# Edge loads of 124 rows instead of 128 in a two-layer graph attention kernel

## What is computed

```python
q = (x @ Wq.T + bq).reshape(N, H, C)
k = (x @ Wk.T + bk).reshape(N, H, C)
v = (x @ Wv.T + bv).reshape(N, H, C)
logits = (q[dst] * k[src]).sum(-1) * (1.0 / np.sqrt(C).astype(np.float32))
m = jax.ops.segment_max(logits, dst, num_segments=N)
e = jnp.exp(logits - m[dst])
denom = jax.ops.segment_sum(e, dst, num_segments=N)
alpha = e / (denom[dst] + 1e-16)
msg = v[src] * alpha[..., None]
out = jax.ops.segment_sum(msg, dst, num_segments=N).reshape(N, HC)
return out + x @ Ws.T + bs
```

## Time and profile before

| what | us |
|---|---|
| median of 3 executions | 3700.6 |
| span of the profiled execution | 3707.0 |
| layer 1, first indirect load of kv to the end of the last | 197.1 to 1338.4 |
| layer 2, the same | 1515.0 to 2666.8 |
| experts, from the first load of `fin_x` | 2701.5 to 3707.0 |
| one indirect load of kv: POOL busy, mean | 1.074 |

### The profile page before, as it was taken

How to read it: one execution, slowest core, us unless ns; L and a number is a source line. 1 busy time by engine, 2 the same in 40 slices (tenths; PEclk the granted TensorE clock), 3 DMA queues, 4 the chain that set the end, 5 groups by cost and what they waited for, 6 DMA issues and landing times. The chain is left out here.

```text
span 3707.0 us, 49221 instructions
## 1 busy us (share of the span) xinstructions
PE 2464.8 (66%) x13243; PEld 2115.8 (57%) x13243; DVE 2398.1 (65%) x3615; ACT 1119.3 (30%) x2130; POOL 2051.4 (55%) x1958
## 2 busy tenths in 40 slices
PE   2435556665656656265656556655569999999999
PEld 1324444554545444154544444444459989989898
DVE  3347777777777764277777777777746556566555
ACT  6301111111111111011111111111146666666665
POOL 6567777777777747677777777777610000000000
PEclk9756666666666655566666666666679999999999
DMA  9334444444444422344444445444310000000000
GB/s 378 112 103 119 125 121 122 125 119 128 119 127 119 124 69 71 87 123 136 124 129 127 125 125 132 124 131 125 97 38 4 23 22 3 23 22 2 21 11 11
DMA packets 394181, 356.62 MB, mean 96 GB/s; under 512 B 88694, under 2 KB 327436, under 8 KB 394080
## 3 DMA queue, kind: packets, MB, share of 16 engines
q1 hardware_dynamic: 221360, 168.40, 15.2%
q0 software_dynamic: 62896, 125.63, 13.6%
q10 hardware_dynamic: 109824, 61.36, 5.4%
HBM read 246.90 MB, written 108.30 MB: 96 GB/s over the span
## 5 line engine op out<-in xcount | busy, mean ns | idle before, releaser
L542 POOL DMA_INDIRECT kv<-kv_table,ix x1664 | 1786.4, 1074 | 531.4 <-issue 497.2
L554 PE MATMUL kT<-identity,kv 128*128 128x128 f32 x832 | 361.3, 435 | 1037.6 <-DMA kv<-kv_table,ix 1037.6
L554 PEld LDWEIGHTS kT<-identity,kv 128*128 128x128 f32 x832 | 182.5, 219 | 1061.1 <-DMA kv<-kv_table,ix 813.4
L650 ACT ACTIVATE ex<-gap 128x1024 f32<-128x1024 f32 x208 | 219.8, 1057 | 1859.4 <-DVE gap L626 1859.4
L604 DVE TENSOR_TENSOR_SCAN held_q<-mask,held_q,qT 128x512 f32<-128x512 bf16 x208 | 266.1, 1280 | 600.4 <-PE qT L555 599.5
L1324 DVE TENSOR_TENSOR hid_lo_x<-full_x,hid_hi_x 128x448 fp32r<-128x448 f32 x448 | 276.2, 622 | 267.8 <-ACT hid_hi_x L1210 264.0
L1210 ACT ACTIVATE full_x<-psH_x,offset_x,scale_x 128x448 f32<-128x448 f32 x448 | 332.5, 742 | 290.6 <-PE psH_x L1065 290.5
L561 PE MATMUL logit<-kq,head_sum 128*128 128x512 f32 x416 | 388.7, 1037 | 1.9 <-DVE gap L626 1.9
L1014 POOL DMA_DIRECT2D x_x<-in_x x7 | 6.8, 974 | 633.6 <-DVE total_x L1368 633.6
L555 PE MATMUL qT<-identity,qz 128*128 128x128 f32 x832 | 347.2, 417 | 0.0
L578 PE MATMUL restT<-pick,top 128*128 128x8 f32 x1664 | 335.4, 274 | 0.0
(11 more groups left out here) (209 smaller groups left out, 5238.8 us busy)
## 6 DMA issues: line engine op xcount, KB each, us to landing
running_sums<-rows ACTq DMA_DIRECT2D x208, 288.0 KB
qz<-q_at_starts SPq DMA_DIRECT2D x208, 256.0 KB, 3.2
mask<-masks SPq DMA_DIRECT2D x416, 128.0 KB, 3.7
q_at_starts<-zeros SPq DMA_DIRECT2D x16, 1664.0 KB, 18.7
kv<-kv_table,ix POOLq DMA_INDIRECT x1664
x_sb<-in_x SPq DMA_DIRECT2D x1, 6272.0 KB, 27.3
kv_table<-proj SPq DMA_DIRECT2D x14, 448.0 KB, 3.3
x_x<-in_x POOLq DMA_DIRECT2D x7, 896.0 KB, 5.7
```

Source lines behind the costliest of these rows:

```text
L542: pool.indirect_dma_start(kv[:, u, j, 2 * HC * s:2 * HC * (s + 1)], None, kv_t, bass.IndirectOffsetOnAxis(ix[:, u, n:n + 1], 0), bounds_ch ...
L554: pe.transpose(kT[u % 2][:, P * j:P * (j + 1)], kv[:, u, j, 0::2], identity[:, :])
```

## The change

A tile of edges is ROWS = 124 edges instead of 128, one to a partition, so partitions 124 to 127 of `ix`, `kv`, `qz` and `rows` are not used. TPB stays 4, so a block is 496 edges of each stream. 106250 edges then need 27 turns of four blocks, 108 blocks a layer instead of 104; the loop keeps its 24 turns, and three turns are written out before it instead of two. All tiles of 512 columns in SBUF become 496 wide, and transposes are of 124 rows or to 124 rows; the PSUM banks stay 512 wide. `q_at_starts` has 107136 rows instead of 106496.

```diff
@@ -40,13 +40,15 @@
 assert NG * GROUP == NT and NG % 2 == 1
 
 STREAMS = 2
-STEP = 512
-TPB = STEP // P
+ROWS = 124
+TPB = 4
+STEP = TPB * ROWS
 UNROLL = 4
 BLOCKS = -(-E // (STREAMS * STEP * UNROLL)) * UNROLL
 STEPS = BLOCKS // UNROLL
 HALF = BLOCKS * STEP
 EP = STREAMS * HALF
+QROWS = -(-EP // P) * P
 ROW = HC + 2 * HEADS
 DEN, MAX = HC, HC + HEADS
 
@@ -59,7 +61,8 @@
 PROJ = 4 * HC
 HTOK = GROUP * P // 2
 GTOK = GROUP * P
-assert STEPS - 2 == len(EXPERT_LAYERS) * EXPERTS
+PEELED = STEPS - len(EXPERT_LAYERS) * EXPERTS
+assert PEELED >= 2
 
 
 def each_group(eng, body):
@@ -92,12 +95,12 @@
     kv_t = nc.dram_tensor("kv_table", [NP, 2 * HC], F32, kind="Internal").ap()
     q_t = nc.dram_tensor("q_table", [NP, HC], F32, kind="Internal").ap()
 
-    qz_t = nc.dram_tensor("q_at_starts", [EP, HC], F32, kind="Internal").ap()
+    qz_t = nc.dram_tensor("q_at_starts", [QROWS, HC], F32, kind="Internal").ap()
     sum_t = nc.dram_tensor("running_sums", [EP, ROW], F32, kind="Internal").ap()
     mask_t = nc.dram_tensor("masks", [STREAMS, BLOCKS, 2 * STEP], BF16, kind="Internal").ap()
 
-    qz_blocks = qz_t.rearrange("(b j p s) c -> b p j (s c)", j=TPB, p=P, s=STREAMS)
-    sum_blocks = sum_t.rearrange("(b j p s) c -> b p j (s c)", j=TPB, p=P, s=STREAMS)
+    qz_blocks = qz_t[0:EP, :].rearrange("(b j p s) c -> b p j (s c)", j=TPB, p=ROWS, s=STREAMS)
+    sum_blocks = sum_t.rearrange("(b j p s) c -> b p j (s c)", j=TPB, p=ROWS, s=STREAMS)
     kv_nodes = kv_t.rearrange("(i p) c -> p i c", p=P)
     q_nodes = q_t.rearrange("(i p) c -> p i c", p=P)
 
...
@@ -450,12 +453,12 @@
                     return phase.enter_context(nc.sbuf_tensor(f"{name}_{layer}", shape, dt))
 
                 def pb(name):
-                    return phase.enter_context(nc.psum_tensor(f"{name}_{layer}", [P, STEP], F32))
+                    return phase.enter_context(nc.psum_tensor(f"{name}_{layer}", [P, 512], F32))
 
                 U = UNROLL
-                ix = sb("ix", [P, U, TPB * STREAMS], I32)
-                kv = sb("kv", [P, U, TPB, STREAMS * 2 * HC])
-                qz = sb("qz", [P, U, TPB, STREAMS * HC])
+                ix = sb("ix", [ROWS, U, TPB * STREAMS], I32)
+                kv = sb("kv", [ROWS, U, TPB, STREAMS * 2 * HC])
+                qz = sb("qz", [ROWS, U, TPB, STREAMS * HC])
                 mask = sb("mask", [P, U, 2, STEP], BF16)
                 held_q = sb("held_q", [P, 2, STEP])
                 kq = sb("kq", [P, 2, STEP])
@@ -465,20 +468,20 @@
                 wv = sb("wv", [P, 2, STEP])
                 run_v = sb("run_v", [P, U, STEP])
                 run_d = sb("run_d", [P, U, STEP])
-                rows = sb("rows", [P, 2, TPB, STREAMS, ROW])
+                rows = sb("rows", [ROWS, 2, TPB, STREAMS, ROW])
                 if layer == 1:
                     w_raw = sb("w_raw", [P, KC * HID])
                 kT = [pb(f"kT{i}") for i in range(2)]
                 qT = [pb(f"qT{i}") for i in range(2)]
                 vT, logit, outT = pb("vT"), pb("logit"), pb("outT")
-                restT = pb("restT")[:, 0:2 * TPB * STREAMS * HEADS].rearrange("p (m j h) -> p m j h", m=2, j=TPB)
+                restT = pb("restT")[0:ROWS, 0:2 * TPB * STREAMS * HEADS].rearrange("p (m j h) -> p m j h", m=2, j=TPB)
 
                 block = phase.enter_context(nc.Block())
 
 
 
                 past = STEPS * layer
-                peeled = 2
+                peeled = PEELED
 
                 def each_step(eng, body):
                     for i in range(past, past + peeled):
@@ -551,20 +554,20 @@
                         pe.wait_ge(q_in[u], 16 * i + 16)
                         wait_past(pe, kq_ready, b - 1)
                         for j in range(TPB):
-                            pe.transpose(kT[u % 2][:, P * j:P * (j + 1)], kv[:, u, j, 0::2], identity[:, :])
-                            ins = pe.transpose(qT[u % 2][:, P * j:P * (j + 1)], qz[:, u, j, :], identity[:, :])
+                            pe.transpose(kT[u % 2][:, ROWS * j:ROWS * (j + 1)], kv[:, u, j, 0::2], identity[0:ROWS, 0:ROWS])
+                            ins = pe.transpose(qT[u % 2][:, ROWS * j:ROWS * (j + 1)], qz[:, u, j, :], identity[0:ROWS, 0:ROWS])
                         ins.then_inc(kq_turned, 1)
 
                     def logits(b, u, i):
                         pe.wait_ge(kq_ready, b + 1)
                         wait_past(pe, gaps_ready, b)
-                        pe.matmul(logit[:, :], head_sum[:, :], kq[:, u % 2, :], start=True, stop=True)\
+                        pe.matmul(logit[:, 0:STEP], head_sum[:, :], kq[:, u % 2, :], start=True, stop=True)\
                             .then_inc(logits_ready, 1)
 
                     def turn_v(b, u, i):
                         wait_past(pe, weighted, b)
                         for j in range(TPB):
-                            ins = pe.transpose(vT[:, P * j:P * (j + 1)], kv[:, u, j, 1::2], identity[:, :])
+                            ins = pe.transpose(vT[:, ROWS * j:ROWS * (j + 1)], kv[:, u, j, 1::2], identity[0:ROWS, 0:ROWS])
                         ins.then_inc(v_turned, 1)
 
                     def turn_results(b, u, i):
@@ -572,10 +575,10 @@
                         pe.wait_ge(d_summed, b + 1)
                         wait_past(pe, copied, 3 * b)
                         for j in range(TPB):
-                            of = slice(P * j, P * (j + 1))
-                            pe.transpose(outT[:, of], run_v[:, u, of], identity[:, :])
+                            of = slice(ROWS * j, ROWS * (j + 1))
+                            pe.transpose(outT[0:ROWS, P * j:P * (j + 1)], run_v[:, u, of], identity[:, :])
                             pe.matmul(restT[:, 0, j, :], run_d[:, u, of], pick[:, :], start=True, stop=True)
-                            ins = pe.matmul(restT[:, 1, j, :], top[:, u, 1 + P * j:1 + P * (j + 1)], pick[:, :],
+                            ins = pe.matmul(restT[:, 1, j, :], top[:, u, 1 + ROWS * j:1 + ROWS * (j + 1)], pick[:, :],
                                             start=True, stop=True)
                         ins.then_inc(out_turned, 1)
 
...
@@ -655,7 +658,7 @@
                         act.wait_ge(out_turned, b + 1)
                         wait_past(act, rows_out[h], 16 * (U // 2 * i + u // 2))
                         flat = rows[:, h, :, :, :].rearrange("p j s c -> p (j s) c")
-                        act.activation(flat[:, :, 0:HC], outT[:, :].rearrange("p (r c) -> p r c", c=HC),
+                        act.activation(flat[:, :, 0:HC], outT[0:ROWS, 0:TPB * P].rearrange("p (r c) -> p r c", c=HC),
                                        ACT.Copy).then_inc(copied, 1)
                         for m, at in enumerate((DEN, MAX)):
                             act.activation(flat[:, :, at:at + HEADS],
@@ -1429,7 +1432,7 @@
     arrays = {
         "x": x,
 
-        "src": np.ascontiguousarray(src.reshape(STREAMS, BLOCKS, TPB, P).transpose(1, 3, 2, 0).reshape(BLOCKS, P, TPB * STREAMS)),
+        "src": np.ascontiguousarray(src.reshape(STREAMS, BLOCKS, TPB, ROWS).transpose(1, 3, 2, 0).reshape(BLOCKS, ROWS, TPB * STREAMS)),
         "dst": dst,
         "prev": np.concatenate([np.full(1, -1, np.int32), dst[:-1]]),
         "samples": np.ascontiguousarray(dst[:SROWS * SCOLS:SCOLS]),
```

More of the change, by code:

```diff
@@ L193, in build @@
             wrap = sb("wrap", [P, P])
-            zeros = sb("zeros", [P, EP * HC // P // 32])
+            zeros = sb("zeros", [P, QROWS * HC // P // 32])
             dst_b = sb("dst_b", [BLOCKS, STREAMS, STEP], I32)
@@ L241, in _ @@
                             sp.dma_start(mask_t[s], mask_b[:, s, :, :].rearrange("b m c -> b (m c)")).then_inc(masks_out, 16)
-                    sp.dma_start(fill[m], zeros[:, :].unsqueeze(1).to_broadcast([P, 32 // FILLS, EP * HC // P // 32])).then_inc(filled[m % len(filled)], 16)
+                    sp.dma_start(fill[m], zeros[:, :].unsqueeze(1).to_broadcast([P, 32 // FILLS, QROWS * HC // P // 32])).then_inc(filled[m % len(filled)], 16)
                 store_tables(sp, projected, GROUP, stored)
@@ L603, in hold_q @@
                         wait_past(dve, q_held, b)
-                        dve.tensor_tensor_scan(held_q[:, h, :], mask[:, u, 0, :], qT[h][:, :],
+                        dve.tensor_tensor_scan(held_q[:, h, :], mask[:, u, 0, :], qT[h][:, 0:STEP],
                                                held_q[:, 1 - h, STEP - 1:STEP], ALU.mult, ALU.add).then_inc(q_held, 1)
@@ L607, in hold_q @@
                         wait_past(dve, logits_ready, b - 1)
-                        dve.tensor_tensor(kq[:, h, :], kT[h][:, :], held_q[:, h, :], ALU.mult).then_inc(kq_ready, 1)
+                        dve.tensor_tensor(kq[:, h, :], kT[h][:, 0:STEP], held_q[:, h, :], ALU.mult).then_inc(kq_ready, 1)
                     def maximum(b, u, i):
@@ L617, in maximum @@
                         dve.wait_ge(logits_ready, b + 1)
-                        dve.tensor_tensor_scan(now, mask[:, u, 1, :], logit[:, :], last,
```

(5 more changed lines are left out.)

## The result

The changed kernel takes 4467.58 us (median of four, 4465.02 to 4470.53) where the kernel before takes 3702.06: ratio 1.207, 95% interval 1.205 to 1.209. That is 766 us slower; 90 were forecast, and the range ended at 3900.

A forecast was written before the change was run, and what follows sets the result against it. POOL's back-to-back indirect loads were taken to bound the edge loops. Profiled 3707.0 + 85 for loads + 4 for layer ends + 1 for the prologue = 3797, or 3790 us (+2.4%) against the median; range 3500 to 3900, 80%.

The forecast's parts named there:

- The bound: In the two edge loops, POOL issues its indirect loads back to back and sets the pace; no compute engine is full.
- More loads, +88: POOL in the edge loops: 1728 loads instead of 1664, 64 more at 1.378 us each, +88 us.
- Fewer rows in each, -2 ns: POOL's indirect loads: 124 rows priced like 128, 1.376 us each instead of 1.378.
- The forecast's own sign for this step: POOL's line 545: forecast wrong if a load's median leaves 0.95 to 1.05 us, or idle exceeds 0.35 us a load.
- The rival that won: POOL's time goes with rows per engine: 31 deep, +200 ns a load, 1.578 us, 4136 us in all; chance 13%.
- the first rival: POOL's loads over fewer engines are cheaper: 24 ns per engine, 291 ns saved, 1.085 us a load; chance 36%.
- Blocks 3% shorter, nothing: DVE, ACT and PE in the loops: 0.6% more work in total, hidden behind POOL, so no cost.
- Narrow qz and stores: Transfers of qz, ix and stores over 124 partitions run on four engines; delay alone does no harm.
- engines fit: Likeliest case: a 124-row load costs POOL as the 128-row one and the DMA engines keep up; 3770 to 3820 us, 41%.
- the 10% for overload: Rival: the four DMA engines are overloaded, so ACT waits for a store two blocks back and POOL for ix; 10%.
- The sign that the forecast named for the four engines: Landing of qz, median 3.2 us before: above 5 if it runs on four engines, unchanged if not.
- Ends of the layers, +4: After POOL's last load: the last store slower by 2.7 us a layer, three tail blocks some 0.7 shorter; +4 us.

The follow-up runs named there:

- the kernel with 128 rows in each load: The changed kernel with only the indirect loads widened again from 124 to 128 rows; 3810.75 us, 1.029 of the kernel before.
- the split kernel: The changed kernel with 128-row loads, and qz and the store each issued as partitions 0 to 111 and 112 to 123; 3799.92 us, ratio 1.026.
- the bench: Separate kernel without the computation: only back-to-back indirect loads of 512-byte rows, eight for each of 16 row counts; 1.00 us a load at 128 rows, 1.38 at 124.

## Why the prediction was wrong

**The bound** was read rightly. POOL's loads set the pace before and after, and their idle time is "issue" in both.

**More loads, +88:** right. In the kernel with 128 rows in each load the 1728 loads take 1838.0 + 569.1 = 2407 us, 89 more than the 2318 of the earlier trace rows. That it fits to 1 us is in part luck: 21 of the 89 are more waits for `ix` and `vT`, and the mean load was 10 ns shorter there (1064), 17 us. In the split kernel, where these waits are as before, it is 84 more.

**Fewer rows in each, -2 ns:** this is the step that failed. The load costs 1372 ns in the median instead of 1007, 1453 in the mean instead of 1074; 1728 x 0.379 = 655 us. Set against the kernel with 128 rows in each load, busy and idle time together are 3061.8 - 2407.1 = 655 us more, the whole gap between 3811 and 4468. The forecast had seen the reason. It read from 29 completions that a transfer over 65 rows runs on 13 engines, gave 124 rows four engines for the queues of SP and ACT, and then costed POOL's own loads as if they kept 16, "by the nearest row". But the nearest row in count (128) was the one that differed in the thing that matters, how the rows divide: the packets show four engines with 31 rows each for POOL's loads too. The forecast's own sign for this step, a median outside 0.95 to 1.05 us, came true; the other, more idle time, did not.

**The rival that won** had 13%: POOL's time goes with the rows that one engine gets. Its mechanism was right and its size half: 8.7 ns a step, from 946 and 1007 ns, where the runs show 15.7 between 1 and 8 deep and, with layer 1's median, (1371 - 1007) / 23 = 15.8 from there to 31. With 15.8, which is taken from the result, it would have said 3790 + 1728 x 0.364 = 4419 us, 1.1% from what was measured. By an estimate from the other rows, the 15.8 is itself two things: some 65 ns that a count not divisible by 16 costs at the same depth (120 rows, 1072 ns), and 13 ns for each of the 23 steps (31 to 127 deep in the bench). The 946 came from single loads, one in a layer. The fixed part of a load also is not work done once for each engine with rows, as the first rival had it: one engine with 31 rows costs 1.32 us, four with 31 each 1.38.

**Blocks 3% shorter, nothing:** right; DVE's busy time is 843 and 853 us in loops of 1518.

**Narrow qz and stores:** four engines each, right by the 4 completions of a store, and for qz and ix by the packets of 4 bytes in q1, which fell from 14774 to 10098; 16 each in 208 blocks before and 4 each in 216 now, with the 256 that 16 masks more bring, would be 4672 fewer, and 4676 are. How much of a block such engines are busy, and whether they are the same four each time, no run shows; the 41% ("engines fit"), the 10% for overload and the time of the cheaper loads, by which the range reaches down to 3500, rest on the author's estimate of it. What the runs show in its place is a cost that is small, about 11 us and not clear of nothing. An overload they don't show: the kernel with 128 rows in each load takes 3811 us where the forecast's sum has 3790, and its waits for `ix` and `vT` grew by 21 us. The sign that the forecast named for the four engines, a landing of qz above 5 us, can't be read: the profile after gives no landing for qz. In the changed kernel itself a block lasts 14 us (1517.8 / 108), where it was 11, and q1 and q10 take 15.8% and 5.0% of the 16 engines' span, against 17.6% and 5.6% in the kernel with 128 rows in each load.

**Ends of the layers, +4:** +7 measured. The experts took 9 us longer than in the first profile of before, but in the second one (3708.2 us in all) they took 1014 us too, so that is not the change.

**The range** left out the case of the deep loads; with it at the 4136 us of its sum, the measured time would still have lain outside. Of three readings of one unknown the range held two, and the third was backed by the rows as well as the first; no row of the trace tells "cheaper" from "deeper", to which it gave 36 and 13%.

## What to carry to other kernels

Keep the partition count of an indirect load divisible by 16, or at least by 15, 14 or 10, as in the 120, 126 and 100 rows tried here (1.06 to 1.07 us); 124 looks almost like 128 and is 31 deep where 128 is 8 (1.38 us against 1.00). Cost such a transfer by the rows that one engine gets, not by rows in all, and look in the queue's packets for how many engines a shape runs on: on the queues of SP and ACT the completions told it here (16 a store over 128 partitions, 4 over 124), on POOL's, which has 16 for every load here, the sizes and number of the data packets did. When a term has no row, list the ways in which the nearest row may differ before taking its value, and take the slope for a back-to-back stream from a stream, not from a single instruction (16 rows: 890 ns in the series, 946 as single loads).

## What the runs showed of the hardware that was not expected

- An indirect load with fewer than 16 shares fills up the other engines: 80 packets a load for 124 rows against 32 for 128, 48 of them with nothing but pieces of 4 bytes (1488 bytes). POOL's loads post 16 completions whatever their rows: 128 in each series of eight, from 16 to 128 rows.
- One row fewer can make a load dearer for POOL: 127 rows took 2.60 us and 128 rows 1.00.
- The store and qz over 124 partitions are cheaper to issue than over 128, on ACT's and on SP's queue: 262 ns in the median for the store against 378, 268 for qz against 383, in the rows of their lines. In the kernel with narrow qz and stores the masks behind them are issued and land later (879 ns for 490, 6.7 us for 3.7). The line of the store after:

```profile
L668 ACTq DMA_DIRECT2D running_sums<-rows x216: 262/262/564, 266.4 to 3444.9; - x108
```
